# A state-space mixer with routed experts: prologue interleaved, expert units moved by one tile, out-projection ahead of the level products

## What is computed

```python
    x = L0_attn_hidden_states
    xn = _layernorm(x, axis=-1)
    s = _L0_attn_ref(xn, ...)                 # mixer
    g = _silu(_L0_ffn_ref(xn, ...))           # experts
    return x + s * g

    # mixer: D_IN 512, HEADS 64 of 8, STATE 128, K 4
    proj = hidden_states @ in_proj_w.T
    gate, xBC, dt = ...                       # 512, 512 + 128 + 128, 64 columns
    conv = conv_b + sum((conv_w[:, i] * xp[:, i:i + l, :] for i in range(K)))
    xBC = jax.nn.silu(conv)                   # x, Bm, Cm
    dt = jax.nn.softplus(dt + dt_bias)
    y = _ssd(x * dt[..., None], dt * A, Bm, Cm)
    y = y + D[None, None, :, None] * x
    hg = y * jax.nn.silu(gate)
    var = jnp.mean(hg * hg, axis=-1, keepdims=True)
    return (hg * jax.lax.rsqrt(var + EPS) * norm_w) @ out_proj_w.T

    # experts: E 8, I 512
    max_ind = jnp.argmax(route, axis=1)
    for e in range(num_experts):
        mask = (max_ind == e)[:, None]
        h = jax.nn.silu(x @ gate_w[e]) * (x @ up_w[e])
        out = out + jnp.where(mask, h @ down_w[e], 0.0)
    return out * max_prob
```

## Time and profile before

| | us |
|---|---|
| median of 3 runs | 482.48 (481.71 to 482.88) |
| the profiled execution | 481.9 |
| its span | 479.8 |

### The profile page before, as it was taken

How to read it: one execution, slowest core, us unless ns; L and a number is a source line. 1 busy time by engine, 2 the same in 40 slices (tenths; PEclk the granted TensorE clock), 3 DMA queues, 4 the chain that set the end, 5 groups by cost and what they waited for, 6 DMA issues and landing times. The chain is left out here.

```text
span 479.8 us, 7469 instructions
## 1 busy us (share of the span) xinstructions
PE 396.2 (83%) x2410; PEld 325.0 (68%) x2410; DVE 322.8 (67%) x691; ACT 198.9 (41%) x492; POOL 215.5 (45%) x252
## 2 busy tenths in 40 slices
PE   0779355519999999999999999999989999997850
PEld 0664113319788787988687889778678879996630
DVE  5506874246599483859598666569698667857678
ACT  1552459411733626351733634541633662262100
POOL 3200571282028362619146546408236537776830
PEclk9958598758999999999999999999999999999995
DMA  8950128522464564777575663855575624313695
GB/s 275 282 135 1 67 99 269 167 81 87 170 186 159 181 176 170 194 217 200 201 212 193 171 201 121 248 172 165 194 207 190 167 92 130 113 56 119 207 338 177
DMA packets 56054, 81.41 MB, mean 170 GB/s; under 512 B 4720, under 2 KB 34416, under 8 KB 55888
## 3 DMA queue, kind: packets, MB, share of 16 engines
q1 hardware_dynamic: 54144, 75.81, 51.3%
q0 software_dynamic: 1872, 5.13, 2.9%
HBM read 64.37 MB, written 16.56 MB: 169 GB/s over the span
## 5 line engine op out<-in xcount | busy, mean ns | idle before, releaser
L580 POOL TENSOR_TENSOR ARENA<-ARENA 128x512 f32<-128x512 f32 (+1 forms) x80 | 104.0, 1308 | 8.4 <-ACT ARENA L788 3.5
L1013 PEld LDWEIGHTS BANK<-ARENA 128*128 128x128 f32 x736 | 87.4, 196 | 23.5 <-ACT ARENA L824 15.8
L1013 PE MATMUL BANK<-ARENA 128*128 128x128 f32 x736 | 89.1, 280 | 16.8 <-ACT ARENA L824 15.6
L632 POOL DMA_INDIRECT gate_rows<-ARENA x23 | 23.0, 1001 | 150.1 <-DVE ARENA L1314 68.7
L905 PE MATMUL BANK<-ARENA,W_MAIN 128*128 128x512 f32 x160 | 76.6, 625 | 14.1 <-DVE ARENA L1210 14.1
L1191 DVE SCALAR_TENSOR_TENSOR ARENA<-BANK,CONVC,ARENA 128x511 f32<-128x511 f32 (+2 forms) x72 | 53.6, 748 | 27.0 <-ACT ARENA L728 14.8
L1046 DVE TENSOR_TENSOR ARENA<-ARENA,BANK 128x256 f32<-128x256 f32 (+1 forms) x128 | 57.3, 448 | 12.5 <-POOL ARENA L646 7.7
L905 PEld LDWEIGHTS BANK<-ARENA,W_MAIN 128*128 128x128 f32 x160 | 30.8, 202 | 49.9 <-issue 31.8
L1046 DVE TENSOR_TENSOR BANK<-BANK,ARENA 128x512 f32<-128x512 f32 (+1 forms) x80 | 50.1, 638 | 6.0 <-PE BANK L954 3.7
L963 PE MATMUL BANK<-ARENA 128*128 128x128 f32 x384 | 48.2, 281 | 6.2 <-POOL ARENA L580 5.3
L963 PEld LDWEIGHTS BANK<-ARENA 128*128 128x128 f32 x384 | 45.2, 194 | 7.0 <-issue 5.1
(11 more groups left out here) (132 smaller groups left out, 643.0 us busy)
## 6 DMA issues: line engine op xcount, KB each, us to landing
ARENA<-source_rows SPq DMA_DIRECT2D x96, 144.0 KB, 2.9
ARENA<-in_w_gate SPq DMA_DIRECT2D x23, 512.0 KB, 4.7
ARENA<-in_w_up SPq DMA_DIRECT2D x23, 512.0 KB, 5.9
ARENA<-in_w_down SPq DMA_DIRECT2D x23, 512.0 KB, 6.8
source_rows<-ARENA SPq DMA_DIRECT2D x16, 288.0 KB, 2.8
ARENA<-in_x SPq DMA_DIRECT2D x8, 512.0 KB, 6.9
ARENA<-x_by_expert SPq DMA_DIRECT2D x23, 129.0 KB, 5.9
ARENA<-gate_rows SPq DMA_DIRECT2D x4, 512.0 KB, 8.3
```

Of the source, the lines that this page charges most:

```text
L580: nc.gpsimd.tensor_tensor(out=XS[par][rows, out_slot, 0:DIN].rearrange("p (a h) -> p a h", a=HD), in0=E2[par][rows, out_slot, :].unsqueeze ...
L632: pool.indirect_dma_start(out=g_dram, out_offset=bass.IndirectOffsetOnAxis(ap=TOKENS[:, t:t + 1], axis=0), in_=FY[par], in_offset=None).th ...
L1013: ins = nc.tensor.matmul(bank[:, f * P:(f + 1) * P], lhsT=WEXP[:, slot, at:at + P], rhs=FXT[par][:, j, :], start=(j == 0), stop=(j == DK - 1))
```

## The change

- In the prologue five of ACT's seven copies in a group go: DVE normalises in place, and the projection reads the transposed tokens that stay anyway. After the groups 1, 2 and 3 one convolution block each is multiplied and copied (`AHEAD`); on DVE the taps of three blocks and the silu products of two stand ahead of the router's chain, one more block stands between it and the ranks. B and C come first (`ORDER`). `W_MAIN` and the taps are loaded earlier.
- The step pair of tile 0 and POOL's carry for the second group stand earlier. ACT no longer waits for the scatter at tile 0's head; SP does, since it issues the loads of the first expert ahead of tile 0's rows, and those of the others behind them.
- The units are 0, 1, 1, eleven times 2, and 1 in tiles 0 to 14 (before: ten times 2 and five times 1).
- sum and tail of the tile before stand ahead of a tile's mid, where tail stood behind the units. The first two finishing steps stand behind the last sum.
- Levels 3 to 5 are read back with the dimension of size 8, 16 or 32 as the outer one.

```diff
+WIDE = 3
+def sources_of(lev):
+    low = times(lev, 0)
+    return low if lev < WIDE else sorted(low, key=lambda t: (t % (1 << lev), t))
...
-ORDER = [*range(HB, BLOCKS), *range(HB)]
+ORDER = [HB + HB, HB + HB + 1, *range(HB, 2 * HB), *range(HB)]
+AHEAD = 3
...
-UNITS = [2] * 10 + [1] * 5
+UNITS = [0] + [1] * 2 + [2] * 11 + [1]
...
-              ("mid", LAST + 3): [("fin", 0, 0), ("fin", 1, 0)],
+              ("sum", LAST + 3): [("fin", 0, 0), ("fin", 1, 0)],
...
-    steps.append(("mid", t, 0))
+    steps += [("tail", t - 1, 0)] * (u > 0) + [("mid", t, 0)]
...
-    steps += [("tail", t - 1, 0)] * (u > 0)
...
-    steps = first[:3] + [("rank", 0, 0)] + first[3:8] + [("sort", 0, 0)] + first[8:] + [
-        ("flush", 0, ORDER[-1]), ("pair", 0, 0), ("head", 0, 0), ("turn", 0, 0)]
+    steps = first[:5] + [("sort", 0, 0), ("rank", 0, 0)] + first[5:9] + [("pair", 0, 0)] + first[9:] + [
+        ("flush", 0, ORDER[-1]), ("head", 0, 0), ("turn", 0, 0)]
...
+                        if lev >= WIDE:
+                            rows = rows.rearrange("q m c -> m q c")
...
+                if kind == "head" and t == 0:
+                    for k in range(1, FXN):
+                        load_rows(k)
+                        if k < WSLOTS:
+                            load_gate_up(k)
+                            load_down(k)
...
-            for k in range(WSLOTS):
-                load_rows(k)
-                load_gate_up(k)
-                load_down(k)
-            for k in range(WSLOTS, FXN):
-                load_rows(k)
+            load_rows(0)
+            load_gate_up(0)
+            load_down(0)
...
                 if kind == "head":
...
-                    if t == 0:
-                        act.wait_ge(scattered, 16 * TILES)
...
+            for g in range(GROUPS):
...
+                if g == 1:
+                    pe.wait_ge(w_loaded, 16)
+                if g > 0:
+                    pe_step(*STEPS[g - 1])
```

More of the change, by code:

```diff
@@ L271, in mixer_moe_kernel @@
         PB = part(NT)
+        rows_at = place[0]
         XS = [part(XSLOTS * RW_X).rearrange("p (l c) -> p l c", l=XSLOTS) for _ in range(2)]
@@ L323, in mixer_moe_kernel @@
         IOTAK = part(TILES)
+        assert place[0] <= rows_at, place[0]
         def rows4(flat, n):
@@ L405, in nth_acc @@
         def nth_acc(q, i):
-            return q * XB + i - HB + 1
+            return q * XB + ORDER.index(i) + 1
         def nth_tanh(q, i):
@@ L625, in pool_step @@
                     sources(0)
-                if kind == "conv" and t % QB and i == HB:
-                    pool.wait_ge(acc_made, nth_acc(t - 1, BLOCKS - 1))
-                    carry(t)
+                if kind == "pair" and t == 0:
+                    carry(1)
+                if kind == "mid" and t % TB == TB - 1 and t + 1 < TILES:
+                    carry(t // GT + 2)
                 if kind == "fy":
@@ L838, in act_step @@
                                          scale=PB[:, t:t + 1]).then_inc(a_moved, 1)
-            act.wait_ge(taps_halved, 1)
-            for s in STEPS[:3]:
+            for s in STEPS[:AHEAD + 1]:
                 act_step(*s)
+            for blk in range(HB):
+                ins = nc.scalar.activation(W_OUT[:, blk, :], W_OUT[:, blk, :], ACT.Copy, scale=NORMC[:, blk:blk + 1])
+            ins.then_inc(w_out_scaled, 1)
             act.wait_ge(v_ready, 1)
@@ L851, in _ @@
             softplus_squares(0)
-            for blk in range(HB):
-                ins = nc.scalar.activation(W_OUT[:, blk, :], W_OUT[:, blk, :], ACT.Copy, scale=NORMC[:, blk:blk + 1])
-            ins.then_inc(w_out_scaled, 1)
-            for s in STEPS[3:]:
+            for s in STEPS[AHEAD + 1:]:
                 act_step(*s)
@@ new lines, in _ @@
+            dve.wait_ge(a_moved, rank + 1)
+            src, step = 0, 1
+            while step < TILES:
+                n = step * EXPERTS
+                nc.vector.tensor_copy(CUM[1 - src][:, 0:n], CUM[src][:, 0:n])
+                link(tt(CUM[1 - src][:, n:], CUM[src][:, n:], CUM[src][:, 0:TE - n], ALU.add))
+                src, step = 1 - src, step * 2
+            count = CUM[src][:, TE - EXPERTS:]
+            link(nc.vector.tensor_scalar_add(CNTI, count, float(P - 1)))
+            link(nc.vector.tensor_single_scalar(CNTS, CNTI, P.bit_length() - 1, ALU.logical_shift_right))
@@ new lines, in _ @@
+            nc.vector.tensor_copy(CNTF, CNTS)
+            link(nc.vector.tensor_copy(ENDS[0], CNTS))
+            esrc, step = 0, 1
+            while step < EXPERTS:
+                nc.vector.tensor_copy(ENDS[1 - esrc][:, 0:step], ENDS[esrc][:, 0:step])
+                link(tt(ENDS[1 - esrc][:, step:], ENDS[esrc][:, step:], ENDS[esrc][:, 0:EXPERTS - step], ALU.add))
+                esrc, step = 1 - esrc, step * 2
+            ends = ENDS[esrc]
+            link(tt(LE.rearrange("p (t e) -> p t e", e=EXPERTS), ends.unsqueeze(1).to_broadcast([P, NT, EXPERTS]),
+                    IOTATF.rearrange("p (t e) -> p t e", e=EXPERTS), ALU.is_le))
@@ new lines, in _ @@
+            link(nc.vector.reduce_sum(EXF, LE.rearrange("p (t e) -> p t e", e=EXPERTS)[:, :, 0:EXPERTS - 1], AX.X))
+            nc.vector.tensor_copy(EXPERT_OF[:, 0:NT], EXF)
+            link(tt(BASE128, ends, CNTF, ALU.subtract))
+            link(nc.vector.tensor_scalar(BASE128, BASE128, float(P), None, ALU.mult))
+            link(tt(R1, RANK, CUM[src], ALU.add))
+            link(tt(R1, R1, TOTS, ALU.subtract))
+            link(tt(by_expert(R1), by_expert(R1), over_tiles(BASE128), ALU.add))
@@ L1356 @@
+            link(tt(R1, R1, HOT, ALU.mult))
+            link(nc.vector.reduce_sum(POSF, by_expert(R1), AX.X))
+            nc.vector.tensor_copy(POS[:, :], POSF).then_inc(routed, 1)
+            for n, s in enumerate(STEPS[AHEAD + 1:]):
+                dve_step(*s)
+                if 2 < n < 7:
+                    first_softplus(2 * (n - 3))
+                    first_softplus(2 * (n - 3) + 1)
 def kernel(**inputs):
```

206 lines of the change are left out of this document (90 added, 116 removed).

## The result

The changed kernel takes **501.4 us** (median of four runs, 499.6 to 506.2) against 482.7 for the kernel before: a ratio of 1.040 (95% interval 1.037 to 1.044). The forecast was 485.6, slower by 3; it is slower by 19. The profiled run took 499.6 us (span 497.5, against 479.8 before).

What follows compares the result with a forecast made beforehand. TensorE was taken to bound 120 to 432 us, chains over several engines the start and last two tiles. +1.2 + 4.7 - 2.8 = +3.1 on the profiled 481.9, 485.0; plus 0.6 for the median, 485.6 us; range 479 to 491.5.

Steps and rivals of the forecast that it cites:

- +1.2: Net us up to tile 3 and its owed units: tile 3 starts 20.9 earlier, but four more expert units cost 22.1.
- -2.8: At the end, POOL's wait of 3.46 us in tile 14 goes, less some 0.7 for ACT's squares; 0 as other bound.
- The out-projection (+4.7, bounds 0 to +10.6): Ahead of level products, PE waits for the sum in tiles 4, 5, 6, 9, 10, less today's waits: net +4.7 us.
- The prologue up to routing: ACT's router exponential ends at 40.5 us; routing ends at 58.5 (56.5 to 63) instead of 50.9.
- The row writes: After routing, tile 0's write takes 3.4 us, tile 1's 4.3; POOL's third pair at 106.8, 1.7 earlier.
- early-routing rival: Full clock through the prologue groups and short DMA queues: exponential ends at 38.6, total 480.2 us; chance 0.2.
- Tile 3: Starts at 158.6 us instead of 179.52, following tile 1's sum at 129.5 and 29.1 us more.
- what would show it: Profile signs: PE waiting 2 to 3 us for the sum in tiles 5, 6, 9, 10; PE fully busy through tile 13.

Runs made afterwards that it cites:

- experiment 1: Changed kernel with the whole out-projection and its sum of squares back behind the level products and second expert unit, first two finishing steps too: 482.3 us, ratio 0.998.
- experiment 2: Kernel before, with only the out-projection and its sum of squares put ahead of the level products, and the two finishing steps moved: 507.1 us, ratio 1.049.
- experiment 7: Changed kernel with unread filler products (7, 5, 6, 4) ahead of PE's wait for the sum in tiles 2, 5, 9, 10: 496.4 us, ratio 1.030.
- experiment 8: Changed kernel with only the one-column product on the sum of squares behind the level products, the four other out-projection products staying ahead: 476.3 us, ratio 0.983.
- experiment 3: Changed kernel with the expert units of before (two in tiles 0 to 9, one in 10 to 14): 488.2 us, ratio 1.012.
- experiment 4: Changed kernel with out-projection place and expert units both put back, leaving the new prologue, load order and row reads: 465.7 us, ratio 0.963.
- experiment 5: Kernel with the prologue alone, given one expert unit in tiles 0 and 1, two in 2 to 12, one in 13: 473.8 us, ratio 0.976.
- experiment 10: Kernel before with only the row reads of levels 3 to 5 changed (source order, constant matrices, sort, small dimension inside): 479.0 us, ratio 0.991.
- experiment 9: Kernel with the prologue alone, with the row reads of levels 3 to 5 put back as before: 476.2 us, ratio 0.985.

## Why the prediction was wrong

The direction and half of the mechanism were named, and one term was mis-sized by far more than its bounds. Experiment 1 measures all the others together: the changed kernel without the new place of the out-projection took 1.0 us less than the kernel before, where +1.2 and -2.8 had forecast 1.6 less. The error of 16 us lies in the remaining term.

**The out-projection (+4.7, bounds 0 to +10.6): the step that failed.** It costs 19 to 20 us in the changed kernel and 24 in the kernel before (experiments 1 and 2). In tiles 4 to 10, for which it was worked out, it is 13.3 by the table. The waits themselves were forecast well there: 10.6 us gross in five tiles, 10.5 in the trace, and 0.9 more at the end of tile 7. So was what returns: 5.9 forecast, and 11.3 + 7.7 - 13.3 leaves 5.7. Two things were missing. (1) The clock. I let every product after a wait run at full speed; the level products of tiles 5, 9 and 10 took 7.7 us more. The bound of +10.6 had no room for that, though rows 6 showed, in the prologue, what follows idle time. (2) The other tiles. Tile 2, tile 12 and the end, for which this term had nothing, hold some 8 us more (experiment 1). DVE stands idle as well (2.56 and 1.31 us in tile 5), but no run shows that this keeps the lag alive from tile to tile: in experiment 7 it idles only 1.49 and 0.45 us there, and the next tile's wait for the sum is the same, 1.95 us against 1.96. Experiments 7 and 8 show the parts: 5 us given back by filling the waits, all of the loss by moving one product of one column.

**The prologue up to routing.** In the profiled execution the exponential ended at 36.0 (forecast 40.5, at best 38.6) and the last cast of routing at 53.5 (58.5; 56.5 to 63). That is only one of two courses. The second group's sixteen matmuls took 2.00 us here and in experiments 3 and 7, but 3.69 in the other eight traces with this prologue. There the exponential ended between 38.9 and 41.2 and the last cast between 56.3 and 58.7, so for most traces this step was right or close. The rows of the changed kernel, with those of experiment 8 for the second group in between:

```profile
19.21 2.00 PE L1043 MATMUL BANK<-W_DR,ARENA 128*128 128x72 f32 x16 [0.69 <-ACT ARENA L700]
...
53.31 0.17 DVE L1371 CAST POS<-ARENA 128x16 uint32<-128x16 f32 x1
```

```profile
19.42 3.69 PE L1045 MATMUL BANK<-W_DR,ARENA 128*128 128x72 f32 x16 [0.69 <-ACT ARENA L700]
```

```profile
79.53 0.50 SPq L474 DMA_DIRECT2D source_rows<-ARENA  x1
85.05 3.70 SPq L484 DMA_DIRECT2D ARENA<-source_rows  x6
...
93.49 0.43 SPq L474 DMA_DIRECT2D source_rows<-ARENA  x1
100.62 3.68 SPq L484 DMA_DIRECT2D ARENA<-source_rows  x6
...
107.64 0.32 POOL L610 TENSOR_TENSOR ARENA<-ARENA 128x64 f32<-128x64 f32 x1
...
129.66 1.03 DVE L1265 TENSOR_REDUCE ARENA<-ARENA 128x128 f32<-128x512 f32 x1
```

The row writes then took 5.5 and 7.1 us where I had 3.4 and 4.3, and gave the 5 us back: POOL's step for the third pair of tile 1 stood at 107.6 (forecast 106.8) and tile 1's sum ended at 130.7 (129.5). Two errors cancelled in this trace, which is luck. Of the early-routing rival's two conditions the full clock came true and the short queues did not, and it did not decide.

**Tile 3.** It began at 161.4 instead of 158.6, and the balance was +3.9 instead of +1.2. In tile 2 I had put no wait. PE waited there for the sum, and the level products behind it took 1.38 and 4.28 us:

```profile
153.93 0.38 PE L995 MATMUL BANK<-CONST,ARENA 128*128 128x1 f32 x2 [3.42 <-DVE ARENA L1265]
```

Rows of the kernel before had warned of it: in its tile 2 the level products begin at 165.56, PE would come to the sum 1.74 later, at 167.3, and the sum ends at 169.2.

```profile
165.56 1.00 PE L954 MATMUL BANK<-ARENA 128*128 128x64 f32 x8
...
168.16 1.03 DVE L1309 TENSOR_REDUCE ARENA<-ARENA 128x128 f32<-128x512 f32 x1
```

How the +3.9 splits is not exact: in experiment 1 tile 2 takes 4.4 us less, but routing ended 3.6 later in that execution, and tile 3 begins at 164.9 against 164.7 (L940). The sum was nearly right and still hid the main thing: I set "20.9 us earlier" against "22.1 us owed" as two effects of one change. Experiments 3 to 5 show that the units can be left where they were. Then tile 3 begins only 4.2 us later, and the whole kernel is 14 to 17 us faster. That the prologue's gain of 17 and the units' cost of 14 to 17 nearly cancel is why the other terms came out so close; neither was forecast by itself. No rival of mine said that the change holds a version faster than before.

**The end (-2.8).** Measured 0.0, but by two effects: with all of the out-projection behind, tile 14 to the end takes 41.2 us instead of 43.9, which is the gain forecast (2.2 of it come from the row reads alone, experiment 10); with it ahead PE waits 8.8 us for the gated rows at three places and the 2.7 are gone. The wait for POOL in tile 14 did vanish.

**Of what would show it**, the waits in tiles 5, 6, 9 and 10 were there (2.55, 1.96, 3.14 and 2.08), tiles 7 and 11 had none ahead of their level products, and tiles 11 to 13 were full (PE busy 62.6 of 63 us).

## What to carry to other kernels

When an instruction is moved ahead in a queue, look for the single operand that is late, and move everything but that: here four of five products ahead were worth 6 us, the fifth cost 25. A wait on the bounding engine costs its length and, where the clock falls, the slower work that follows: here 9.4 us on top of 16.4. And take the parts of a change apart before adding them up: an expert unit of 5.5 us that stood in the stretch where PE waited anyway cost about 4 us more once it was moved to tiles that PE bounds.

## What the runs showed of the hardware

After a wait of 2.55 us between full-clock products the same level products (24 passes of 128x128) took PE 4.91 us instead of 2.90, at a granted clock of 0.57. The length of the wait alone doesn't decide it. Here is tile 6, in the changed kernel and then in experiment 7:

```profile
260.63 0.38 PE L995 MATMUL BANK<-CONST,ARENA 128*128 128x1 f32 x2 [1.96 <-DVE ARENA L1265]
...
261.80 2.90 PE L963 MATMUL BANK<-ARENA 128*128 128x128 f32 x24
```

```profile
255.28 0.38 PE L997 MATMUL BANK<-CONST,ARENA 128*128 128x1 f32 x2 [1.95 <-DVE ARENA L1267]
256.45 4.52 PE L963 MATMUL BANK<-ARENA 128*128 128x128 f32 x24
```

The waits are equal; in one kernel the products ran at 2.4 GHz (granted clock 1.00), in the other mostly at 1.2 (0.61). What else tells the two apart stays open. Nor does the program alone decide it: in the prologue the same sixteen matmuls after the same 0.69 us of waiting took 2.00 us in three traces and 3.69 in eight, and routing ended some 3 to 5 us later for it. (The granted clock that the profile gives there reads 1.00 for both; in the kernel before, rows of 3.69 us stand at 26.6 and 33.4 us with 0.50.) Times in the first tiles that come from one trace carry this difference.

The order of dimensions in 144 KB reads changed what others got. Their own median time to landing stayed (2.9 us old, 3.1 new), that of the experts' rows fell from 8.4 to 4.9 us and of the down weights from 7.9 to 5.1 (experiment 9 against 4); in the kernel before the falls are smaller, 5.9 to 5.3 and 6.8 to 5.3 (against experiment 10). One reading is that a few of the sixteen engines had long queues and held up transfers that were spread over all of them. It was not tested by itself.
